# Attention kernel on one core: row sums inverted in two groups, two residuals and one value part moved, blocks of the third output moved

## The reference, cut to what matters

```python
# part 1: group norm, attention over the 1024 positions, projection, residual
xn = group_norm(x); q, k, v = qkv_w @ xn + qkv_b
attn = softmax(q.T @ k / sqrt(C)); x = x + proj_w @ (attn @ v) + proj_b
# part 2: layer norm over channels, attention with squared cosines
t = tokens(x); u = layer_norm(t); n = u / |u|
t = t + softmax((n @ n.T) ** 2) @ u
# part 3: layer norm, product with sign(weight) * scale, clip and round, residual
y = layer_norm(t) @ sign_weight + bias; t = t + round(clip(y, -1, 1) * 7) / 7 (+ bias)
```

## Time and profile before

| | value |
|---|---|
| runs, median of 3 | 1683.55 us |
| the profiled execution | 1684.76 us |
| its span in the trace | 1683.0 us |
| granted TensorE clock, mean | 0.999 |
| period of one batch in the loop (L620 waits at 698.30 and at 801.26) | 103 us |

### The profile page before, as it was taken

The page is one execution under the profiler, slowest core; times in us unless marked ns, Lnnn a source line. Parts: engine busy times, 40 slices in busy tenths (PEclk is TensorE's granted clock), DMA queues, the critical chain, the costliest instruction groups (busy, mean ns, idle before and its releaser), DMA issues.

```text
span 1683.0 us, 33368 instructions
## 1 busy us (share of the span) xinstructions
PE 1637.0 (97%) x10994; PEld 1504.9 (89%) x10994; DVE 1373.0 (82%) x2695; ACT 993.1 (59%) x1588; POOL 733.7 (44%) x1078
## 2 busy tenths in 40 slices
PE   7999999999999999999999999999999999999997
PEld 6888989989899998999989999898998989989896
DVE  6779787887878879788797887978879787887877
ACT  3665755656565565755657556565565656556563
POOL 1362534525354263533626346253452535526351
PEclk9999999999999999999999999999999999999999
DMA  5545546455454654646455463554645545464443
GB/s 147 163 126 182 155 151 166 146 180 145 153 156 153 196 141 139 162 148 192 131 162 160 151 187 120 179 148 152 174 138 182 152 145 162 150 188 130 138 133 93
DMA packets 218750, 259.86 MB, mean 154 GB/s; under 512 B 30176, under 2 KB 188256, under 8 KB 218720
## 3 DMA queue, kind: packets, MB, share of 16 engines
q1 hardware_dynamic: 218720, 259.48, 52.1%
HBM read 138.81 MB, written 120.59 MB: 154 GB/s over the span
## 4 chain that ended last, share of the span: by engine, by line
PE 35%; issue 24%; POOL 16%; DVE 15%; ACT 8%; DMA 1%; POOLq 1%; DVEq 0%; SPq 0%; ACTq 0%
PE wide L482 11%; DVE neg_max L1179 4%; POOL root_pair L1525 3%; PE turn L650 3%; PE turn L652 3%; PE narrow L650 3%; PE turn L651 3%; PE narrow L652 3%; PE narrow L651 3%; PE narrow L482 3%; DVE x_norm L1243 2%; POOL val L1544 2%; POOL len_i L1538 2%; DVE prob L1251 2%; POOL var_pair L1520 2%
## 5 line engine op out<-in xcount | busy, mean ns | idle before, releaser
L857 ACT ACTIVATE expo<-wide,neg_max 128x1024 f32<-128x1024 f32 x128 | 143.1, 1118 | 263.5 <-DVE neg_max L1179 263.5
L482 PE MATMUL wide<-xn_hi,prob 128*128 128x512 f32 x1024 | 295.9, 395 | 1.1 <-ACT expo L857 1.1
L482 PEld LDWEIGHTS wide<-xn_hi,prob 128*128 128x128 f32 x1024 | 187.6, 188 | 42.2 <-ACT expo L857 1.2
L1568 POOL TENSOR_TENSOR carrier_p<-ones 128x1 f32<-128x1 f32 x60 | 11.7, 195 | 363.4 <-DVE y_sb L1296 360.9
L1188 DVE STREAM_TRANSPOSE x_norm<-expo 128x1024 f32<-128x1024 f32 x112 | 139.4, 1244 | 32.9 <-ACT expo L857 30.0
L1179 DVE TENSOR_REDUCE neg_max<-wide 128x1 f32<-128x1024 f32 x128 | 155.0, 1211 | 12.3 <-PE wide L482 12.2
L482 PE MATMUL wide<-xn_lo,prob 128*128 128x512 f32 x512 | 160.7, 394 | 0.0
L650 PE MATMUL turn<-val,prob 128*128 128x258 f32 x512 | 146.9, 287 | 13.5 <-DVE prob L1251 13.5
L1552 POOL TENSOR_TENSOR prob<-expo,prob 128x128 fp32r<-128x128 f32 (+6 forms) x112 | 144.6, 1298 | 29.3 <-DVE prob L1228 29.3
L1520 POOL TENSOR_TENSOR var_pair<-ln_mv,eps_or_none 128x4 f32<-128x4 f32 x64 | 30.6, 477 | 275.0 <-DVE ln_mv L1216 275.0
L1193 DVE TENSOR_TENSOR prob<-e_back,prob 128x1024 fp32r<-128x1024 f32 x112 | 136.1, 1215 | 16.2 <-ACT prob L864 16.0
(11 more groups left out here) (184 smaller groups left out, 5226.2 us busy)
## 6 DMA issues: line engine op xcount, KB each, us to landing
e_scratch<-x_norm SPq DMA_DIRECT2D x112, 512.0 KB, 3.0
e_back<-e_scratch SPq DMA_DIRECT2D x448, 128.0 KB, 3.1
x_raw<-in_x SPq DMA_DIRECT2D x32, 512.0 KB, 3.7
e_back<-in_x SPq DMA_DIRECT2D x64, 256.0 KB, 5.0
out<-y_sb SPq DMA_DIRECT2D x64, 256.0 KB, 3.2
ln_scratch<-x_norm SPq DMA_DIRECT2D x30, 512.0 KB, 3.0
expo<-ln_scratch SPq DMA_DIRECT2D x120, 128.0 KB, 2.8
e_scratch<-x_norm SPq DMA_DIRECT2D x32, 448.0 KB, 2.6
```

The lines of the kernel that those rows point to most:

```text
L482: mm = pe.matmul(o, lhsT, r, start=first and i == 0, stop=last and i == len(parts) - 1)
L857: act.activation(expo[:, n % DEEP], wide[n % 2][:, :], ACT.Exp, bias=neg_max[:, n:n + 1], accum_out=row_sum1[:, n:n + 1]).then_inc(e1_made, 1)
```

## The change

Four edits:

1. DVE: the eight reciprocals inside residual1 (one column each) go. `inverse_sums(b, h)` inverts four columns at once: group 0 behind e1T_lo(b, 0), once exponentials 0 to 3 are there; group 1 behind e1T_lo(b, 4), once all eight are there. residual1 waits for it instead (inv1_made in place of t1_steps).
2. DVE: residual1(b, 2) moves ahead of cosT_lo(b, 0), and residual1(b, 3) right behind it; both were behind e1T_lo(b, 5).
3. POOL: value_lo(b, 1) moves ahead of layer_norm1(b, 2).
4. PE: the eight blocks of output 2 leave product2(b, 2). Blocks 2 to 5 go into products2_end ahead of block (1, 0), blocks 6, 7, 0, 1 to its end. The wait for the last group of values goes from the start of products2_end to behind blocks 2 to 5.

```diff
-                dve.reciprocal(inv_sum1[:, n:n + 1], row_sum1[:, n:n + 1]).then_inc(t1_steps, 1)
-                dve.wait_ge(t1_steps, i + 1)
+                dve.wait_ge(inv1_made, 2 * b + n // HT + 1)
...
+            def inverse_sums(b, h):
+                rows = slice(HT * h, HT * (h + 1))
+                dve.wait_ge(e1_made, NT * b + HT * (h + 1))
+                dve.reciprocal(inv_sum1[:, rows], row_sum1[:, rows]).then_inc(inv1_made, 1)
...
                 e1T_lo(b, 0)
+                inverse_sums(b, 0)
                 e1_turn(b, 3)
...
                 e1T_lo(b, 4)
+                inverse_sums(b, 1)
+                residual1(b, 2)
                 cosT_lo(b, 0)
+                residual1(b, 3)
                 e1T_lo(b, 5)
-                residual1(b, 2)
-                residual1(b, 3)
...
-                pe.wait_ge(val_made, N1 * b + N1)
+                pe.wait_ge(val_made, N1 * b + N1 - 1)
                 for j in range(2, NT):
                     if j == NT - 2:
+                        for i in range(2, j):
+                            product2_block(b, 2, i, 2, 1)
+                        pe.wait_ge(val_made, N1 * b + N1)
                         product2_block(b, 1, 0, 1, 7)
...
+                for j in (NT - 2, NT - 1, 0, 1):
+                    product2_block(b, 2, j, 2, 1)
...
-                for n in range(2, NT):
+                for n in range(3, NT):
                     product2(b, n)
...
                 lengths(b, 1)
+                value_lo(b, 1)
                 layer_norm1(b, 2)
                 lengths(b, 2)
-                value_lo(b, 1)
```

More of the change, by code:

```diff
@@ L245, in build @@
         pv1_up = sem("pv1_up")
-        t1_steps = sem("t1_steps")
+        inv1_made = sem("inv1_made")
         t1_made = sem("t1_made")
@@ L813, in _ @@
             products2_end(f)
-            for n in range(2, NT - 1):
+            for n in range(3, NT - 1):
                 product2(f, n)
```

## The result

The changed kernel takes 1656.68 us, the median of 4 runs (1656.18 to 1657.21), beside 1683.45 for the kernel before: ratio 0.984, 95% interval 0.9827 to 0.9852, so the gain is clear of the noise. The forecast was 1657.0. The medians differ by 26.8 us, where the sum had said 26.4. The profiled execution took 1657.21 with a span of 1655.5, against 1684.76 and 1683.0 before, 27.5 us less.

The account below looks back on a forecast made before the run. PE, busy 97% of the span, was taken as the bound, so only its waits could change. 12.5 + 16.6 - 1.2 - 1.5 = 26.4 us off 1684.76 gives 1658.4, or 1657.0 on the median's scale; range 1653.5 to 1667.

Parts of the forecast that it names:

- Wait A: PE's wait for the unit rows at turn_cos's transposes, 0.91 late per batch, would go: gain 12.5 us.
- The new waits of edit 1: DVE's four-column reciprocal of group 0 would delay PE's product1(1) by 0.08 per batch, 1.2 us in 15.
- Wait B: PE's wait for the turned triangle at block (1, 0), 1.08 per batch, would go by moving blocks: gain 16.6 us.
- The start of the next batch: At scores1(0) a stall of about 0.1 per batch would stay, DVE moving up less than PE: 1.5 us in 15.
- Edit 3 and the last batch: Moving value_lo(1) on POOL costs PE nothing; the last batch gains nothing at block (1, 0).
- two charges: The losses set against the gains: 1.2 us at product1(1) and 1.5 us at scores1(0).
- The end does not follow: Rival: squares, triangle fetches and next normalisation keep their place, stalling scores1(0) some 1.0: 15 us in all, 1672; chance 0.08.
- A wait stays: Rival: group 2's unit rows or triangle row 7 replace Wait A or Wait B in full: 1669.5 or 1673.6; chance 0.07.
- The shared port: Rival: value_lo(1) on POOL holds up DVE beside residuals 4 and 5, 0.5 per batch, 7.5 us: 1664.5; chance 0.1.
- Slower: Rival: DVE's moved work and e1T_lo(5) run stretched 2.3 times, stalling PE at product1(5): 26 us slower, 1709; chance 0.03.
- No change: Rival: the waits only move, because DVE and not PE sets the period: 1683; chance 0.03.

Follow-up runs that it names:

- the run with two delays: The changed kernel with two useless DVE maxima over 1024 columns (2.3 us) ahead of cosT_lo(0): 1671.34 us, ratio 0.9912 to the kernel before.

## Why the prediction was right, and where its reasons were not

**The bound and the two waits.** Right. PE's work stayed, its waits were all that moved. From the first queries to the last, 15 turns, 26.7 us went, 1.8 per turn; the trace has neither wait in the loop. (The sum's own terms give 1657.15, written as 1657.0.)

**Wait A.** That it goes is right, and the new order fell as worked out: reciprocal and residual 2 in the first hole, residual 3 in the second, e1T_lo(5) in place, ACT at once, 2.1 to spare where 1.8 was forecast, group 2 ready at 691.44 for 692.13. That edit 2 is what removes it was half the truth. Edit 2 alone gives 12.9 us, the 12.5 of the sum; but edit 1 alone gives 14.7 and takes 0.71 of A's 0.87, and with edits 1, 3 and 4 in place edit 2 is worth 1.35. The step that failed is the sentence that residuals 0 and 1 lose their reciprocals "though PE is not waiting there". Residual 0 stands ahead of the transposition whose fetch feeds e1T_lo(5), and e1T_lo(5) stood at the head of the chain behind wait A.

**The new waits of edit 1.** The charge of 1.2 us at product1(1) did not come. The four-column reciprocal is shown as 0.17, but the next row starts 0.08 behind it, and the slack was 0.08:

```profile
756.31 0.17 DVE L1210 RECIPROCAL inv_sum<-row_sum 128x4 f32<-128x4 f32 x1
756.39 1.21 DVE L1193 STREAM_TRANSPOSE x_norm<-expo 128x1024 f32<-128x1024 f32 x1
```

By starts product1(1) is not late in any batch. A row's duration is not its price in a queue whose next row doesn't depend on it. In the sum edit 1 stood as a cost; it is the edit that is worth most by itself.

**Wait B.** Gone, as forecast. But the 16.6 us put down to edit 4 are too much for it. With edits 1 and 2 in place 1667.40 was left; the changed kernel, which ran on other chips, takes 1656.7 to 1658.4. So 9 to 11 us are edit 4's. Alone it gives 10.5, because some 0.4 per batch comes back at scores1(0). The rest of the wait went with edit 1: B is 0.55 shown with it and 0.75 with edit 2 alone. The way is seen in all runs. From group 2's transposes on PE to the triangle on DVE it was 14.36 us (702.70 to 717.06) and is 14.15 (692.13 to 706.28), and residual 7, a link of that chain, has lost its reciprocal. The means of the loop are 14.36 to 14.39 in the four kernels without edit 1 and 14.15 to 14.18 in the ten with it. Residual 7's scaling starts 0.2 earlier beside PE in these ten, and behind it the chain takes 15.0 in all but one (15.1 without edit 2): the reciprocal is the 0.2. For the last 0.1 of the 0.3 by starts no link is named here. The sum had this chain move with PE only.

**The start of the next batch.** A stall was rightly placed at scores1(0). By starts it cost 1.9 us in all, where 1.5 was put: 0.6 in the first full turn, 0.2 to 0.3 in three others, 0.14 or less in the rest. Without edit 1 it is 4.9, so its size depended on an edit that the sum had not tied to it.

**Edit 3 and the last batch.** As forecast, no price and no gain, but only because edit 2 brings group 1 forward: without it value_lo(1) holds up group 2. In the last batch the wait for ACT's rows at turn_ln2 is 1.15, as before.

**Why the total held.** A and B can each go only once. Single effects of 14.7, 12.9 and 10.5 add up to 38; the measured total is 26.8 to 27.5, bounded by the two waits, 2.0 per batch. The sum was built on the waits, so it was right; the shares of the edits were not. That 26.4 came so close has some luck in it: of its two charges, 2.7 together, one did not come and the other came to 1.9.

**The rivals.** *The end does not follow*: out, B's triangle and row 7 moved up with PE and more. *A wait stays*: out, the smallest room left is 0.7 and 0.8. *The shared port*: its time, 1664.5, did not come, nor do the rows show it. value_lo(1) runs at 684.97 beside residual 5 and the end of residual 4, and residual 5's rows stay at 0.47 and 0.43. What was stretched is ln_shift on POOL, 1.16 for 0.2, while DVE's e1T_lo(6), which reads two operands in SBUF, ran at 681.81. The Trainium skill ("SBUF — State Buffer", section "Who interferes with whom") says that a VectorE instruction with two inputs in SBUF and a GpSimd instruction that reads SBUF exclude each other, and that one with a single SBUF input does not contend. The trace agrees with both: ln_shift is the first case, and value_lo(1) beside residual 5, which reads one tensor from PSUM and one from SBUF, the second. *Slower*: out, and the run with two delays shows that its place was real: e1T_lo(5) 0.9 us later is free, 2.0 later costs 0.85. *No change*: out.

## What to carry to other kernels

Where the busiest engine is at 97%, list its waits in a period: their sum bounds what any reordering can give, and single edits must not be added beyond it. For each edit follow also the engines on which "nobody waits": a few small instructions with a wait for themselves, one of them ahead of a transfer, were worth four fifths of a wait that another edit was thought to remove. Do not take the list of waits for their sum: here 1.9 us stood in waits of which it listed one of 0.3. And before the new slack is called comfortable, look one stage on, at the first operation of the next turn, and at which other queue sits in front of it.

## What the runs showed of the hardware

A reciprocal of one column followed by an instruction that waits for it delays that instruction by 0.19 to 0.37 us, and one of four columns whose result the next instruction does not need delays it by 0.08. A GpSimd instruction of 0.2 us took 1.16 beside a VectorE instruction with two SBUF operands. The kernel before differs by 5.4 us between two chips (1680.50 and 1685.89). The changed kernel differs by 1.8 between them (1656.61 without edit 3, and 1658.40). Two chips do not show why.
